# A Mamba block with experts on one core: the front's convolution put on TensorE, stores by parts, and one subtraction moved from POOL to VectorE

## The chip, the core and the metric

The kernel runs on one core of a Trainium2 chip. A core has five engines, each with its own instruction queue: TensorE (PE in the rows; PEld is its weight loads), VectorE (DVE), ScalarE (ACT), GpSimd (POOL) and SyncE (SP), which here only issues DMAs. They wait for one another by semaphores. SBUF is the working memory of 128 partitions; TensorE writes into PSUM, eight banks of 128x512 f32. The metric is the time of one execution in microseconds (us) on the device; lower is better.

## The reference, cut to what matters

The input x is (4, 1024, 128). First a Mamba block, then a layer norm, then four expert layers (4 experts, two chosen per token) and another norm. Only the start of the Mamba block concerns this change:

```python
xn = (x - mu) * rsqrt(var + 1e-05) * ln_w + ln_b
xi, z = split(xn @ W_in, 2)              # 256 channels each
xc = causal depthwise convolution of xi over time, 4 taps   # per channel
u = silu(xc + conv_b)
x_dbl = u @ W_xproj                      # dt_r (8), B (64), C (64)
delta = softplus(dt_r @ W_dt + b_dt)
# then, step by step over time, for every channel d and state n:
#   h = h * exp(delta * A) + (delta * u) * B ;  y = sum_n h * C
y = (y + u * D) * silu(z);  out = x + y @ W_out
```

A depthwise convolution has one weight per channel and tap: xc[t, d] is the sum over j of w[d, j] * xi[t - 3 + j, d].

## The kernel before

The program has three stages: the front (about 210 us), which computes u, silu(z), delta, delta*u, B and C for all tokens and stores them in DRAM; the scan stage, in which VectorE runs 512 scans of 128x1040 elements, with ScalarE and TensorE preparing their inputs; and the expert layers.

**The front** works on items: item k is one batch row's 512 tokens (`TT`), there are 8 (`ITEMS`, `LAST` = 7), and buffers are doubled, `bb = k % 2`. Channels lie on the partitions in two halves of 128 (`HALVES`). Each engine has its own list of work, written out by hand in the order in which it is to run; the loop over k is unrolled. Per item:

- VectorE: moments of x (`input_moments`), normalising it (`input_norm`); `convolve`: for each tap and half one 128x512 instruction, 8 in all (L1298 for tap 0, L1300 for the others), then the last three columns are copied to the front of the buffer `xi` as the next tile's history (L1311), or zeroed (L1313) where the row starts anew; `steps(k-1)`: delta and delta*u (L1319, 1322, 1324); `remainder(k-1)` (L1329, 1331); relu of the softplus argument (L1367), the copy of C (L1373), 1+exp (L1376), its rounding error (L1378), B's high part and its rest (L1385, 1387). The loop's order is: convolve, moments(k+2), steps(k-1), norm(k+2), remainder(k-1), relu, C, softplus, B.
- TensorE: `turn_x` transposes xn (L1015), `inner` multiplies with W_in's first 256 columns (L1024), `gate_of` with the others (L1033); x_dbl = first part of the projection, 72 rows (L1058); `turn_du` transposes delta*u (L1044); `v` is dt_r @ W_dt (L1067); B by token (L1073). Order in the loop: x_dbl(k), turn_du(k-1), v(k), B(k), gate_of(k+1), turn_x(k+2), inner(k+2). Operands are f32; the trace shows two records for each f32 matmul of 512 columns.
- ScalarE: `take_xnT` evacuates the transposed xn with the norm's scale and bias (L842), `take_xi` evacuates inner's result (L850); silu(z) (L877), u = silu(convolution + bias) in two halves (L882), first part of delta (L857), dt_r (L889), first part of delta*u (L862), abs (L897), exp (L901), second part (L867), logarithm (L905). Silu, exp and logarithm need different tables: three table loads an item.
- POOL: the power -0.5 of the norm (L629); `last_part(k-1)` (L674); middle and low part of B (L700, 702); and some clearing of the scan stage's buffers.
- SP: the DMAs, in a written order, too.

**Parts.** delta and delta*u (128x2048 f32 together) are stored as three bf16 numbers that add up to the f32: part 0 is the rounded value (ScalarE), `rest` what is left of it (VectorE), part 1 the rounded rest (ScalarE), part 2 is rest minus part 1 (POOL, L674). Semaphores `a_p0`, `a_p1`, `a_p2` count the items whose part is done. `store_parts(k)` waits for part 2 and then issues 12 DMAs of 256 KB: pairs 0, 1, 2 are part 0, pairs 3 and 4 part 1, pair 5 part 2, each pair for delta (`dl_d`) and delta*u (`du_d`). In item k's turn SP does: load x(k+3), store u and silu(z), store C (`c_d`), store_parts(k-1), store B's six pairs. `a_rows[bb]` counts the landed stores; the first scan of the second block (L1439) and buffer reuse wait for it.

**Waits around the change.** The convolution waits for `a_xi` and, two items later, for `a_u` (its output buffer `conv`); u waits for `a_conv`; take_xi for `a_padded`; x_dbl (L1056) for `a_u`; turn_x(k) for C and dt_r of item k-2, whose PSUM bank it reuses; inner(k) also for `a_brest` of item k-2 (the bank of B); gate_of(k) for `a_rest` of item k-2.

Of the kernel before, what the change touches and what calls it, by code (L numbers as in the profile page):

```python
# [11 lines left out]
P = 128  # L12
# [32 lines left out]
def build(nc, x, vecs, chan, a_log, ident, w_in, w_xproj, w_dt, w_out,  # L45
# [18 lines left out]
    with ctx:  # L64
# [96 lines left out]
        wdt_s = take(DI)  # L161
        assert at_[0] <= GD * SEG
# [7 lines left out]
        dd, rest, slip, lg, sz_s, conv, part, b_part = ([None, None] for _ in range(8))  # L170
# [19 lines left out]
        xnT = [take(TT) for _ in range(2)]  # L190
# [10 lines left out]
        xi = [take(HALVES, KC - 1 + TT) for _ in range(2)]  # L201
# [3 lines left out]
        conv = [take(HALVES, TT) for _ in range(2)]  # L205
# [69 lines left out]
        a_padded = sem("a_padded")  # L275
# [9 lines left out]
        a_xi = sem("a_xi")  # L285
        a_pad = sem("a_pad")
        a_conv = sem("a_conv")
# [23 lines left out]
        a_tap = sem("a_tap")  # L311
# [133 lines left out]
        def _(sp):  # L445
# [17 lines left out]
            load_x(0)  # L463
            load_x(1)
# [47 lines left out]
            for k in range(ITEMS):  # L512
# [26 lines left out]
                if k > 0:  # L539
                    store_parts(k - 1)  # L540
# [4 lines left out]
            store_parts(LAST)  # L545
# [71 lines left out]
        def _(pool):  # L617
            for bb in range(2):
                last = nc.gpsimd.memset(xi[bb][:, :, 0:KC - 1], 0.0)
# [56 lines left out]
            for k in range(ITEMS):  # L676
# [7 lines left out]
                if k == LAST:  # L684
# [4 lines left out]
                    pool.wait_ge(a_conv, ITEMS)  # L689
# [6 lines left out]
                if k > 0:  # L696
                    last_part(k - 1)
# [134 lines left out]
        def _(act):  # L832
# [4 lines left out]
            def take_xnT(k):  # L837
# [7 lines left out]
            def take_xi(k):  # L845
                bb = k % 2
                act.wait_ge(a_xip, k + 1)
                if k > 1:
                    act.wait_ge(a_padded, k - 1)
                nc.scalar.activation(xi[bb][:, :, KC - 1:], PS[:, 4 * bb:4 * bb + 2, :], ACT.Identity).then_inc(a_xi, 1)  # L850
# [857 lines left out]
```

## Time and profile before

| | us |
|---|---|
| three runs, median (lowest to highest) | 2373.51 (2368.64 to 2374.96) |
| the profiled execution | 2374.5 |
| its span, first to last instruction | 2372.7 |
| front, to the first scan | 213 |
| VectorE / TensorE / ScalarE / POOL busy, whole span | 2068.1 / 2152.9 / 1520.5 / 977.3 |

The profile is of one execution. It lists each instruction with its engine, its line, output and inputs, and the idle time before it with the engine that ended it; merged rows carry a count. Idle time of an engine that is not the bound costs nothing; busy shares over the whole span mix three stages with different limits, so the front has to be read by itself.

### The profile page before, as it was taken

How to read it: one execution, taken by the hardware profiler on the slowest of the kernel's cores; microseconds unless marked ns; L12 is line 12 of the kernel's file. 1: busy time of each engine (PE TensorE's matmuls, PEld its weight loads, DVE VectorE, ACT ScalarE, POOL GpSimd, SP SyncE). 2: the span in 40 equal slices, each digit the busy share in tenths (PEclk: the TensorE clock that was granted, in tenths of full speed). 3: DMA queues.
4: the chain of work that ended last, by engine and by line, in shares of the span. 5: the costliest groups of instructions: out<-in, count | busy, mean ns of one | idle time of the engine just before them, and what ended most of it. 6: DMA issues, size and time to landing. Idle time of an engine off the chain costs nothing. (4 is left out here: it accounts for less than half of the span.)

```text
span 2372.7 us, 49889 instructions
## 1 busy us (share of the span) xinstructions
PE 2152.9 (91%) x16864; PEld 1275.1 (54%) x16864; DVE 2068.1 (87%) x2937; ACT 1520.5 (64%) x1795; POOL 977.3 (41%) x475
## 2 busy tenths in 40 slices
PE   6675999999999999999999965999999999989987
PEld 3331333333333333333333324888899989989876
DVE  7987999999999999999999956777877787787776
ACT  5666888888888888888888841343344334434332
POOL 4325344444434434344343424444444544444342
PEclk7665999999999999999999986999999999999998
DMA  4777212212222122221222231000100020000000
GB/s 114 224 225 222 49 40 49 45 40 44 43 45 46 39 44 44 45 46 38 47 45 42 46 104 52 1 0 0 36 1 0 1 72 1 0 1 6 9 4 18
DMA packets 354411, 114.38 MB, mean 48 GB/s; under 512 B 282968, under 2 KB 345056, under 8 KB 354080
## 3 DMA queue, kind: packets, MB, share of 16 engines
q1 hardware_dynamic: 349584, 110.26, 19.0%
q10 hardware_dynamic: 4752, 3.15, 0.4%
q8 instruction: 43, 0.70, 0.1%
q14 instruction: 32, 0.26, 0.0%
HBM read 67.45 MB, written 45.88 MB: 48 GB/s over the span
## 5 line engine op out<-in xcount | busy, mean ns | idle before, releaser
L1442 DVE TENSOR_TENSOR_SCAN arena<-behind 128x1040 f32<-128x1040 f32 x512 | 1156.9, 2309 | 9.8 <-ACT behind L927 6.2
L997 ACT ACTIVATE arena<-PS,arena 128x512 f32<-128x512 f32 x512 | 348.3, 689 | 544.7 <-PE PS L1210 543.8
L917 ACT ACTIVATE behind<-PS 128x1024 f32<-128x1024 f32 x512 | 526.7, 1029 | 133.8 <-DVE arena L1442 101.1
L1126 PE MATMUL PS<-arena 128*32 128x128 f32 x8192 | 566.1, 406 | 1.8 <-DVE arena L1442 1.8
L927 ACT ACTIVATE behind<-PS 128x1024 f32<-128x1024 f32 x512 | 539.2, 1053 | 7.5 <-PE PS L1109 3.8
L1222 PE MATMUL PS<-arena 128*128 128x128 f32 x4096 | 483.8, 278 | 23.2 <-DVE arena L1591 23.0
L1222 PEld LDWEIGHTS PS<-arena 128*128 128x128 f32 x4096 | 480.5, 195 | 34.4 <-DVE arena L1591 22.7
L715 POOL COPY behind<-carry 128x64 f32<-128x64 f32 x128 | 209.7, 1639 | 514.7 <-DVE arena L1442 374.0
L1210 PE MATMUL PS<-parts_xh,parts_w 128*128 128x512 f32 x1536 | 391.1, 409 | 25.8 <-DVE parts_w L1468 15.3
L1126 PEld LDWEIGHTS PS<-arena 128*32 128x32 f32 x8192 | 235.4, 119 | 290.7 <-issue 212.6
L1109 PE MATMUL PS<-arena 96*128 96x512 bf16 x1024 | 314.9, 390 | 53.8 <-ACT behind L927 35.1
L1210 PEld LDWEIGHTS PS<-parts_xh,parts_w 128*128 128x128 f32 x1536 | 292.2, 196 | 86.2 <-DVE parts_w L1468 15.9
L1096 PE MATMUL PS<-arena,Ast 96*128 96x512 bf16 x1024 | 315.1, 390 | 3.9 <-ACT behind L917 3.9
L1503 DVE SCALAR_TENSOR_TENSOR arena<-arena 128x128 f32<-128x128 f32 x164 | 189.3, 1215 | 46.0 <-POOL arena L629 46.0
L1109 PEld LDWEIGHTS PS<-arena 96*128 96x128 bf16 x1024 | 67.5, 98 | 266.6 <-ACT behind L927 249.3
L781 POOL TENSOR_TENSOR arena<-euler,arena 128x16 f32<-128x16 f32 x32 | 92.6, 2894 | 220.3 <-DVE arena L1532 220.3
L1096 PEld LDWEIGHTS PS<-arena,Ast 96*128 96x128 bf16 x1024 | 58.6, 98 | 230.8 <-ACT behind L917 198.9
L1591 DVE SCALAR_TENSOR_TENSOR arena<-PS,arena 128x128 f32 (+1 forms) x512 | 144.0, 344 | 28.9 <-PE PS L1222 19.2
L629 POOL TENSOR_TENSOR arena<-arena,neg_half 128x4 f32<-128x4 f32 x49 | 53.9, 1101 | 241.5 <-DVE arena L1268 241.5
L789 POOL TENSOR_TENSOR arena<-arena 128x2048 f32<-128x2048 f32 x32 | 147.4, 4606 | 12.8 <-POOL arena L629 12.8
L798 POOL TENSOR_TENSOR arena<-arena 128x2048 f32<-128x2048 f32 x32 | 115.6, 3612 | 77.8 <-DVE arena L1562 75.3
L729 POOL COPY arena<-arena 64x64 f32<-64x64 f32 x64 | 129.8, 2028 | 11.8 <-POOL behind L715 9.7
(120 smaller groups left out, 1451.7 us busy)
## 6 DMA issues: line engine op xcount, KB each, us to landing
dl_d<-arena SPq DMA_DIRECT2D x48, 256.0 KB, 3.5
du_d<-arena SPq DMA_DIRECT2D x48, 256.0 KB, 3.6
arena<-dl_d SPq DMA_DIRECT2D x512, 24.0 KB
arena<-b_d SPq DMA_DIRECT2D x64, 192.0 KB
arena<-du_d SPq DMA_DIRECT2D x512, 24.0 KB
b_d<-arena SPq DMA_DIRECT2D x48, 128.0 KB, 2.9
u_d<-behind SPq DMA_DIRECT2D x8, 512.0 KB, 3.7
sz_d<-arena SPq DMA_DIRECT2D x8, 512.0 KB, 4.7
```

The costliest lines, as they stand in the source:

```text
L715: nc.gpsimd.tensor_copy(seg(dB[:, G_])[:, :, 0], carry[:, pair, d:d + GD]).then_inc(slot_ready, 1)
L789: nc.gpsimd.tensor_tensor(scored, X[:, bass.ds(g * GT, GT), :].unsqueeze(2).broadcast_to([P, GT, E, H]), rw_s[:, bass.ds(l, 1)].broadcast_ ...
L917: nc.scalar.activation(seg(dA[:, half])[:, :, 1:], PS[:, 0:2, :].rearrange("p j (i t) -> p (j i) t", t=TC), ACT.Exp).then_inc(exp_done, 1)
L927: nc.scalar.activation(seg(dB[:, G_])[:, :, 1 + 2 * OCT * r:1 + 2 * OCT * (r + 1)], PS[:, 2:4, :].rearrange("p o (t d) -> p d (o t)", d=GD ...
L997: nc.scalar.activation(hT[:, e % 2, c], PS[:, HIDDEN[(GT * e + c) % 3], :], ACT.Gelu, bias=bias1[:, lp, e * GT + c:e * GT + c + 1]).then_i ...
L1096: last = nc.tensor.matmul(PS[:, j, :], Ast[0:ROWS, kk * (DB // GI) + 2 * q + j, :], rhs_d[kk][0:ROWS, 2 * q + j].rearrange("r i t -> r (i ...
L1109: last = nc.tensor.matmul(PS[:, 2 + oct_ % 2, :], Bst[kk][0:ROWS, oct_, :], rhs_u[kk][0:ROWS, oct_, :, G_ * GD:(G_ + 1) * GD], start=True, ...
L1126: last = nc.tensor.matmul(PS[32 * j:32 * j + 32, 4 + kk, 0:DB], cd[:, pair, j, 32 * i:32 * i + 32], seg(hb[kk])[:, :, 1 + 16 * j + i], sta ...
L1210: last = nc.tensor.matmul(PS[:, HIDDEN[(GT * e + c) % 3], :], w1p[:, lp, part_w, e, c * P:(c + 1) * P], xhT[:, gp, part_x], start=(part_w ...
L1222: last = nc.tensor.matmul(PS[:, 2 + e % 2, s * P:(s + 1) * P], hT[:, e % 2, c, s * P:(s + 1) * P], w2_s[:, lp, e * GT + c], start=(c == 0) ...
L1442: nc.vector.tensor_tensor_scan(hb[kk][:, q * QD * SEG:(q + 1) * QD * SEG], dA[:, q % 2], dB[:, G_, lo:lo + QD * SEG], 0.0, ALU.mult, ALU.a ...
L1503: last = nc.vector.scalar_tensor_tensor(dst(s), src(s), mv[:, s, 0:1], rs[:, s:s + 1].broadcast_to([P, H]), ALU.subtract, ALU.mult)
```

## The change

- `convolve`, `take_xi` and their buffers go. The convolution is folded into the projection: `wtap[:, t]` = W_in's first 256 columns times tap t of each output channel, four weight sets made once by VectorE; the taps come in as a new input, repeated on all 128 partitions (128x1024 f32, 512 KB). `inner(k, h)` adds four matmuls on the transposed xn, shifted by one column each, into one PSUM bank. xnT gets three columns of history in front, which ScalarE fills before it takes the next xnT (a copy, or zeros).
- `inner` is split: its first half stands after turn_du(k-1), its second after v(k), for item k+1, one item later than before.
- u is taken by ScalarE straight out of PSUM, ahead of silu(z).
- SP stores each part when it is ready; part 0's six DMAs stand ahead of the store of C.
- `last_part(k-1)` is done by VectorE at the end of its turn, but for the last item, which stays on POOL.

```diff
@@ SP
-            def store_parts(k):
+            def store_part(k, w):
                 it, bb = k // 2, k % 2
-                sp.wait_ge(a_p2, k + 1)
-                for p in range(PAIRS):
-                    src = part[bb][X_PART[p]]
+                sp.wait_ge((a_p0, a_p1, a_p2)[w], k + 1)
+                for p in [p for p in range(PAIRS) if X_PART[p] == w]:
+                    src = part[bb][w]
...
             load_x(0)
+            sp.dma_start(taps_s.rearrange("p t d -> p (t d)"), taps).then_inc(taps_in, 16)
             load_x(1)
...
+                if k > 0:
+                    store_part(k - 1, 0)
                 sp.wait_ge(a_bc, k + 1)
                 sp.dma_start(c_d[it, bb], bc_t[bb][0:N]).then_inc(c_stored[bb], 16)
...
                 if k > 0:
-                    store_parts(k - 1)
+                    store_part(k - 1, 1)
+                    store_part(k - 1, 2)
...
-            store_parts(LAST)
+            for w in range(PARTS):
+                store_part(LAST, w)
@@ POOL
-                if k > 0:
-                    last_part(k - 1)
@@ ACT
                 if k > 1:
                     act.wait_ge(a_zp, k - 1)
-                nc.scalar.activation(xnT[bb], PS[:, 4 * bb, :], ACT.Identity, bias=vecs_s[:, 1:2],
+                    if k // 2 % 2:
+                        nc.scalar.activation(xnT[bb][:, 0:KC - 1], xnT[bb][:, TT:], ACT.Identity).then_inc(a_halo, 1)
+                        act.wait_ge(a_halo, k // 4 * 2 + bb + 1)
+                    else:
+                        nc.scalar.activation(xnT[bb][:, 0:KC - 1], ident_s[:, 0:KC - 1], ACT.Identity, scale=0.0)
+                nc.scalar.activation(xnT[bb][:, KC - 1:], PS[:, 4 * bb, :], ACT.Identity, bias=vecs_s[:, 1:2],
                                      scale=vecs_s[:, 0:1]).then_inc(a_xnT, 1)
...
             for k in range(2):
                 take_xnT(k)
-                take_xi(k)
             for k in range(ITEMS):
                 bb = k % 2
                 if k > 1:
                     act.wait_ge(a_stored[bb], A_STORES * (k // 2))
+                    act.wait_ge(a_du, k - 1)
+                act.wait_ge(a_xip, HALVES * (k + 1))
+                for h in range(HALVES):
+                    last = nc.scalar.activation(u_s[bb][:, h], PS[:, 4 * bb + h, :], ACT.Silu,
+                                                bias=chan_s[:, h, KC:KC + 1])
+                last.then_inc(a_u, 1)
                 act.wait_ge(a_zp, k + 1)
                 nc.scalar.activation(sz_s[bb], PS[:, 4 * bb + 2:4 * bb + 4, :], ACT.Silu).then_inc(a_sz, 1)
-                act.wait_ge(a_conv, k + 1)
-                if k > 1:
-                    act.wait_ge(a_du, k - 1)
-                for h in range(HALVES):
-                    last = nc.scalar.activation(u_s[bb][:, h], conv[bb][:, h], ACT.Silu, bias=chan_s[:, h, KC:KC + 1])
-                last.then_inc(a_u, 1)
-                if 0 < k < LAST:
-                    take_xi(k + 1)
@@ PE
-            def inner(k):
+            def inner(k, h):
                 bb = k % 2
-                pe.wait_ge(a_xnT, k + 1)
-                if k > 1:
+                if h == 0:
+                    pe.wait_ge(a_xnT, k + 1)
+                elif k > 1:
                     pe.wait_ge(a_brest, k - 1)
-                for h in range(HALVES):
-                    last = nc.tensor.matmul(PS[:, 4 * bb + h, :], win_s[:, h * P:(h + 1) * P], xnT[bb],
-                                            start=True, stop=True)
+                for t in range(KC):
+                    last = nc.tensor.matmul(PS[:, 4 * bb + h, :], wtap[:, t, h * P:(h + 1) * P],
+                                            xnT[bb][:, t:t + TT], start=(t == 0), stop=(t == KC - 1))
                 last.then_inc(a_xip, 1)
...
-            for k in range(2):
-                turn_x(k)
-                inner(k)
+            pe.wait_ge(a_pad, 1)
+            pe.wait_ge(a_wtap, KC)
+            turn_x(0)
+            for h in range(HALVES):
+                inner(0, h)
             gate_of(0)
+            turn_x(1)
...
                     turn_du(k - 1)
+                if k < LAST:
+                    inner(k + 1, 0)
...
                 last.then_inc(a_v, 1)
+                if k < LAST:
+                    inner(k + 1, 1)
...
                 if k < ITEMS - 2:
                     turn_x(k + 2)
-                    inner(k + 2)
@@ DVE
+            dve.wait_ge(weights, WEIGHTS)
+            dve.wait_ge(taps_in, 16)
+            for t in range(KC):
+                nc.vector.tensor_tensor(wtap[:, t], win_s[:, 0:DI], taps_s[:, t], ALU.mult).then_inc(a_wtap, 1)
...
-                convolve(k)
...
+                if k > 0:
+                    dve.wait_ge(a_p1, k)
+                    nc.vector.tensor_tensor(part[1 - bb][2], rest[1 - bb], part[1 - bb][1], ALU.subtract
+                                            ).then_inc(a_p2, 1)
             steps(LAST)
```

## Rows read from the trace of the kernel before

**Rows 1.** Busy time of the engines, clock and DMA in one item's stretch
```profile
core 0: us, PE busy (x) PEld busy (x) DVE busy (x) ACT busy (x) POOL busy (x), PEclk, DMA share, GB/s
106.00:130.00 24.00, 16.79 (x44) 8.11 (x44) 21.37 (x35) 15.74 (x17) 7.10 (x5) 0.64 0.78 226
```

**Rows 2.** VectorE in order of time: start, length, line, output<-inputs, count, idle before
```profile
106.72 3.69 DVE L1298 TENSOR_SCALAR arena<-arena,chan_s 128x512 f32<-128x512 f32 x2
110.44 4.60 DVE L1300 SCALAR_TENSOR_TENSOR arena<-arena,chan_s 128x512 f32<-128x512 f32 x6
...
123.25 1.22 DVE L1329 TENSOR_TENSOR arena<-arena 128x1024 f32<-128x1024 f32 x1 [1.82 <-ACT arena L862]
...
130.15 0.42 DVE L1387 TENSOR_TENSOR behind<-PS,arena 128x256 f32<-128x256 f32 x1
130.49 3.53 DVE L1298 TENSOR_SCALAR arena<-arena,chan_s 128x512 f32<-128x512 f32 x1
...
134.59 1.01 DVE L1300 SCALAR_TENSOR_TENSOR arena<-arena,chan_s 128x512 f32<-128x512 f32 x1
```

**Rows 3.** ScalarE in order of time, the same item
```profile
115.08 1.33 ACT L882 ACTIVATE behind<-arena,chan_s 128x512 f32<-128x512 f32 x2 [4.00 <-DVE arena L1300]
...
124.17 1.27 ACT L897 ACTIVATE arena<-PS,chan_s 128x512 f32<-128x512 f32 x2 [0.95 <-PE PS L1067]
125.45 1.28 ACT L901 ACT_TABLE_LOAD   x1
126.74 1.06 ACT L901 ACTIVATE arena<-arena 128x1024 f32<-128x1024 f32 x1
127.70 1.89 ACT L867 ACTIVATE arena<-arena 128x2048 bf16<-128x2048 f32 x1
...
131.87 0.76 ACT L842 ACTIVATE arena<-PS,vecs_s 128x512 f32<-128x512 f32 x1
...
139.20 1.33 ACT L882 ACTIVATE behind<-arena,chan_s 128x512 f32<-128x512 f32 x2 [4.23 <-DVE arena L1300]
```

**Rows 4.** TensorE in order of time, the same item
```profile
116.47 3.69 PE L1058 MATMUL PS<-behind 128*72 128x512 f32 x4 [3.89 <-ACT behind L882]
120.55 1.61 PE L1044 MATMUL PS<-ident_s,arena 128*128 128x128 f32 x8 [0.40 <-DVE arena L1324]
122.09 1.98 PE L1067 MATMUL PS<-behind 8*128 8x512 f32 x4
124.00 2.70 PE L1073 MATMUL PS<-behind 128*128 128x64 f32 x16
126.49 2.94 PE L1033 MATMUL PS<-arena,behind 128*128 128x512 f32 x4
129.27 0.60 PE L1015 MATMUL PS<-ident_s,arena 128*128 128x128 f32 x4
132.69 3.78 PE L1024 MATMUL PS<-arena,behind 128*128 128x512 f32 x4 [2.82 <-ACT arena L842]
```

**Rows 5.** POOL: its third part, and B's middle part
```profile
129.68 4.06 POOL L674 TENSOR_TENSOR arena<-arena 128x2048 bf16<-128x2048 f32 x1 [10.93 <-ACT arena L867]
133.68 0.60 POOL L700 CAST arena<-behind 128x256 bf16<-128x256 f32 x1
```

**Rows 6.** The start of the front: TensorE, then ScalarE
```profile
8.70 1.11 PE L1015 MATMUL PS<-ident_s,arena 128*128 128x128 f32 x4 [8.70 <-DMA lb_s<-in_ln_b]
...
16.24 1.98 PE L1024 MATMUL PS<-arena,behind 128*128 128x512 f32 x4 [0.93 <-ACT arena L842]
...
21.52 1.32 ACT L882 ACTIVATE behind<-arena,chan_s 128x512 f32<-128x512 f32 x2
...
41.08 1.33 ACT L882 ACTIVATE behind<-arena,chan_s 128x512 f32<-128x512 f32 x2 [1.39 <-DVE arena L1300]
```

**Rows 7.** The end of the front: ScalarE's last u, VectorE's second block
```profile
186.72 1.33 ACT L882 ACTIVATE behind<-arena,chan_s 128x512 f32<-128x512 f32 x2 [4.89 <-DVE arena L1300]
...
238.25 22.26 DVE L1442 TENSOR_TENSOR_SCAN arena<-behind 128x1040 f32<-128x1040 f32 x10 [1.09 <-DMA du_d<-arena]
```

More of the change, by code:

```diff
@@ L42, with build @@
 NG = NT // GT
[L45 removed]
+def build(nc, x, vecs, chan, taps, a_log, ident, w_in, w_xproj, w_dt, w_out,
           router_w, router_b, ln_g, ln_b, w1, b1, w2, b2, out):
@@ L161, in build @@
         wdt_s = take(DI)
+        wtap = take(KC, DI)
         assert at_[0] <= GD * SEG
@@ L169, in build @@
         space[0], limit[0] = arena, ARENA
-        dd, rest, slip, lg, sz_s, conv, part, b_part = ([None, None] for _ in range(8))
+        dd, rest, slip, lg, sz_s, part, b_part = ([None, None] for _ in range(7))
         at_[0] = 0
@@ L189, in build @@
         xn = [take(4, H) for _ in range(2)]
-        xnT = [take(TT) for _ in range(2)]
         sz_s[0] = take(HALVES, TT)
@@ L200, in build @@
         at_[0] = LOWER + HB
-        xi = [take(HALVES, KC - 1 + TT) for _ in range(2)]
+        xnT = [take(KC - 1 + TT) for _ in range(2)]
         sz_s[1] = take(HALVES, TT)
@@ L204, in build @@
         at_[0] = LOWER + HB + RD
-        conv = [take(HALVES, TT) for _ in range(2)]
+        taps_s = take(KC, DI)
         slip[0] = take(HALVES, TT)
@@ L618, in _ @@
             for bb in range(2):
-                last = nc.gpsimd.memset(xi[bb][:, :, 0:KC - 1], 0.0)
+                last = nc.gpsimd.memset(xnT[bb][:, 0:KC - 1], 0.0)
             last.then_inc(a_pad, 1)
@@ L1032, in gate_of @@
                 for h in range(HALVES):
-                    last = nc.tensor.matmul(PS[:, 4 * bb + 2 + h, :], win_s[:, (2 + h) * P:(3 + h) * P], xnT[bb],
+                    last = nc.tensor.matmul(PS[:, 4 * bb + 2 + h, :], win_s[:, (2 + h) * P:(3 + h) * P], xnT[bb][:, KC - 1:],
                                             start=True, stop=True)
@@ L1287, in input_norm @@
                 scaled(lambda s: xt[bb][:, s], mv_a[:, bb], rs_a[:, bb], lambda s: xn[bb][:, s], 4).then_inc(a_xn, 1)
-            def convolve(k):
-                bb = k % 2
-                dve.wait_ge(a_xi, k + 1)
-                if k > 1:
-                    dve.wait_ge(a_u, k - 1)
-                for t in range(KC):
-                    for h in range(HALVES):
-                        tap = chan_s[:, h, t:t + 1]
-                        if t == 0:
-                            last = nc.vector.tensor_scalar(conv[bb][:, h], xi[bb][:, h, t:t + TT], tap, None, ALU.mult)
-                        else:
-                            last = nc.vector.scalar_tensor_tensor(conv[bb][:, h], xi[bb][:, h, t:t + TT], tap,
-                                                                  conv[bb][:, h], ALU.mult, ALU.add)
-                    if t < KC - 1:
-                        last.then_inc(a_tap, 1)
-                        dve.wait_ge(a_tap, k * (KC - 1) + t + 1)
-                    else:
-                        last.then_inc(a_conv, 1)
-                dve.wait_ge(a_conv, k + 1)
-                pad = xi[bb][:, :, 0:KC - 1]
-                if k // 2 % 2 == 0:
-                    nc.vector.tensor_copy(pad, xi[bb][:, :, TT:]).then_inc(a_padded, 1)
-                elif k < ITEMS - 2:
-                    nc.vector.memset(pad, 0.0).then_inc(a_padded, 1)
             def steps(k):
@@ L1685 @@
                                 halves(L0_attn_b_dt), halves(L0_attn_D)], 2),
+        "taps": np.concatenate([f(L0_attn_conv_w).reshape(DI, KC).T.reshape(1, KC * DI)] * P, 0),
         "a_log": f(L0_attn_A_log),
```

18 lines of the change are left out of this document (4 added, 14 removed).

## The prediction

> **What bounds the kernel now.** I read the page's slices first (the front is the first tenth of the span), then the busy time of each engine in one item's stretch, then that item on VectorE, ScalarE and TensorE in order of time. An item is one 512-token tile; there are eight, k = 0 to 7, and the middle ones take 24.1 us each, the spacing of the two u activations in [rows 3] (115.08 and 139.20). In that stretch VectorE is busy 21.4 us of 24, ScalarE 15.7, TensorE 16.8, at a mean granted clock of 0.64, which is mostly the lower of its levels (1.2 of 2.4 GHz) [rows 1]. VectorE is the bound: its only long idle stretch is 1.8 us [rows 2], and ScalarE's u waits 4.0 to 4.2 us for the last tap of the convolution [rows 3]. The convolution costs it 3.7 + 4.6 us in an item [rows 2]. Its first two instructions, single-input operations on 128x512, are stretched: one of them alone took 3.53 us and ended at 134.02, beside POOL's third part, which ran from 129.68 to 133.74 [rows 2, 5]. TensorE waits 2.8 us for xnT and about 4 us for u [rows 4]. After the eighth item the front runs out into the scans; there only the second block's first scan waits for the stores, by 1.09 us [rows 7]. From then on VectorE scans without a gap (10 in 22.3 us [rows 7]) that the front could fill, so whatever brings that scan forward moves the end by as much.
>
> **The change part by part.** *VectorE loses* the convolution and the pad copy, 3.7 + 4.6 + 0.1 = 8.4 us an item, the copy of six columns taken at 0.1, *and gains* the third part: one subtraction of 128x2048, f32 and bf16 in, bf16 out. The nearest row is the same kind of subtraction on 128x1024, 1.22 us [rows 2], so 2.3 us (twice 1.22 less one start-up; above, 2.44). Busy time goes from 21.4 to about 15.3 us: VectorE stops being the bound, if nothing stretches the new instruction.
>
> *POOL* loses 4.06 us an item [rows 5], and with it what held VectorE's single-input operations. It keeps the middle and low part of B. These now start when the third part does, on the other engine. A three-operand instruction of VectorE beside such a POOL operation took 1.01 us where six of its kind took 4.60 together [rows 2]; so I add 0.3 us, 2.6 in all. In the schedule below VectorE has about 1 us of slack there: behind the third part are queued the moments of item k+2 and steps(k), and ScalarE's next wait for delta is also a wait for x_dbl. Cost: nothing up to about 3 us of length, then one for one. The Trainium skill, page SBUF — State Buffer, section Who interferes with whom, says more: the ports that VectorE and GpSimd share are an exclusive lock, and a VectorE instruction with two SBUF inputs contends with a GpSimd instruction that reads SBUF. By that rule the third part could wait out a whole POOL operation rather than 0.3 us, which is the third rival; the 3.53 us in [rows 2] agrees with a lock, and the 1.01 us speaks for a short wait only.
>
> *TensorE gains* three more matmuls for each half, each two records: inner goes from 4 records to 16. Four records took 3.78 us at the low level and 1.98 us at the high one, each with the drain of the last [rows 4, 6]; so one half of an item, 8 records, takes 7.2 or 3.7 us. The idle time of 2.8 us in front of inner and the 4 us before x_dbl are to be judged by the new chain, and that is two legs.
>
> Leg A, from the start of x_dbl(k) to the end of v(k), on TensorE: x_dbl 3.7 (it stands behind an idle stretch, as now, and ran at the low level), turn_du 1.6, the first half of inner(k+1), v 2.0 [rows 4]. In the trace v already runs at the high level, after 5.3 us of x_dbl and turn_du; so I take the half of inner at 3.7. Sum 11.0, less three overlaps of about 0.2 between listed ends and next starts = 10.4. Where the clock is still high at x_dbl this would be 1.7 less. I take 10.0.
>
> Leg B, from there to the next x_dbl, on ScalarE: abs 1.27, table 1.28 (the load is as long each of the three times), exp 0.96 to the next start, second part 1.92, table 1.28, logarithm 0.96 (an instruction like exp's), the new copy of three columns, xnT 0.77, table 1.28, u 1.33 [rows 3]. The copy of three columns has no row; it is bounded by nothing and by the 0.76 us of xnT's 512 columns [rows 3], and a line through that row and exp's (1024 columns, 1.06) leaves 0.46 for no columns at all, of which 0.1 overlaps with the next instruction; as xnT is the dearer form (it reads a scale and a bias), I take 0.25. Sum 11.3. Beside it TensorE does the second half of inner 3.7, B 2.7, the gate 2.9, turn_x 0.6 [rows 4] = 9.9, which fits, though barely: xnT(k+2) waits for that turn_x, and u(k+1) stands behind xnT on ScalarE. So xi's evacuation (1.0 us) goes, and the wait for the convolution goes, but what was hidden beneath it, three table loads included, now lies on the path. The spacing is 10.0 + 11.3 = 21.3 us; I take 21.4. VectorE (15.3) and DMA (0.78 of 24 = 18.7 us of traffic, unchanged in bytes [rows 1]) are below it.
>
> *The start* is later. u(0) begins at 21.52 [rows 6]. New: the taps, 512 KB, are queued ahead of the second x and of the weights, at 225 GB/s [rows 1] up to 2.3 us; TensorE's first work at 8.70 [rows 6] would slip by 0 to 2.3, I take 1.0. The four products for wtap then cost VectorE 4 x 0.42 (the 128x256 row of [rows 2]) = 1.7. From 11.4: turn_x 1.1, xnT 0.8, sixteen records of which four to eight low = 9.2 to 10.9, I take 10; gate 2.0; turn_x(1) 1.0; xnT(1) 0.8, because ScalarE now takes xnT(0) and xnT(1) before anything else; table 1.3. That is 28.4, less overlaps of 0.7 = 27.7: 6.2 us later. The first spacing was 19.6 (21.52 to 41.08 [rows 6]), as item 0 has no predecessor's parts; I take 20.0.
>
> *SP.* A part's stores are released one by one: six after the first part, four after the second, two after the third. The first six are moved ahead of c_d; what is queued behind their wait is c_d and everything after it. c_d is waited for two items later, so this costs nothing. At the end only two stores are left after POOL's last third part, instead of twelve; the 1.09 us wait of block 1 [rows 7] goes. What is late next there are the eight scans of block 0, which do not change.
>
> *Sum.* u(0) to u(7) now: 186.72 - 21.52 = 165.2 us [rows 6, 7]. After: 20.0 + 6 x 21.4 = 148.4. So -16.8, start +6.2, end -1.1: -11.7 us. The profiled execution took 2374.5 (span 2372.7), so 2362.8; the median of the three runs is 1.0 below the profiled one, so 2362.0 when rounded. Scans and expert layers are untouched.
>
> **The rivals.** *Slower: the low clock reaches the convolution.* If leg A's half of inner runs at the low level (7.2 in place of 3.7), leg A is 13.9, the spacing 25.2 to 25.4, and the total 20 + 6 x 25.3 - 165.2 + 6.2 - 1.1 = +11.7: 2386. The place is the first half of inner, behind the idle stretch before x_dbl; the point from which it decides is a spacing of 23.4 us (leg A of 12.1), where the whole change is nothing. For it: after its idle stretch of 2.8 us the inner at 132.69 ran wholly low [rows 4], and an idle stretch of 3.5 us before x_dbl stays (xnT, table, u). Against it: the work after it is denser than before, with 8 records in one piece twice an item, and v was at the high level. 0.13.
>
> *Faster: the clock stays high.* x_dbl 2.0, turn_du 1.0, leg A 8.2, spacing 19.5 to 20; total 20 + 6 x 19.8 - 165.2 + 6.2 - 1.1 = -21.3: 2353. For it: TensorE is now busy some 18 of 20 us; against it: the idle stretch. 0.12.
>
> *The third part is stretched.* If it waits for both of POOL's operations on B, each about as long as the 0.60 us one [rows 5], it is 2.3 + 1.2 = 3.5, 0.5 beyond the slack, in about seven items -4 of the gain; a stretch to the 4.06 us that POOL needed would give back 1 more an item. 2366 to 2371. 0.12.
>
> *Nothing is gained.* The chain closes another way, for instance because SP's stores or the loads in items 4 and 7 set the spacing at about 23.4: 2374. 0.10.
>
> **How the numbers follow.** The forecast of -7 to -16 us has 0.53 and is the likeliest, 2362. A measurement of this kernel tells about 0.3%, 7.1 us, from no change. Faster by more: 0.53 + 0.12 and a part of the third rival, 0.70. Within: the rest of the third and the fourth, 0.17. Slower: 0.13. The range has to leave out no more than 2 in 10: from 2350 (the high-clock case and 3 us of spread, the runs lying 6.3 apart) to 2376 (no gain, and spread), which leaves out the slow rival and little else.
>
> **What would show it.** Right: no convolution on VectorE, its busy share of an item near 15 us; u starts 21 to 22 us apart; a third part of 2.3 to 2.6 us; u(0) at 27 to 28; ScalarE from abs to u without a wait but for turn_x's; block 1's first scan at about 226 and waiting for no store. Wrong: inner's first half above 5 us in most items; a third part above 3; ScalarE waiting for delta longer than for x_dbl; TensorE waiting for wtap beyond 13; or a spacing that follows from SP.

## The result, and the profile after

The changed kernel takes 2363.67 us, the median of 7 runs (2362.76 to 2364.74); the kernel before took 2371.76, the median of 7 runs beside them (2368.64 to 2374.96). The ratio is 0.9965, 95% interval 0.9956 to 0.9975: faster by 8.1 us, where 11.7 were forecast. The profiled execution took 2364.13 us, its span is 2362.3 (before 2372.7).

The page of the changed kernel: the engines' busy time, then VectorE's busy share and the granted clock in 40 slices.

```profile
PE 2162.7 (92%) x16960; PEld 1276.8 (54%) x16960; DVE 2026.2 (86%) x2878; ACT 1513.0 (64%) x1793; POOL 960.9 (41%) x468
...
DVE  4768999999999999999999956777877787787776
...
PEclk9895999999999999999999986999999999999999
```

VectorE lost 41.9 us of work (it had 2068.1), all in the front, the first four digits. The clock there is 9, 8, 9, 5; the kernel before had 7, 6, 6, 5.

The same stretch as [rows 1], and one item from u(4) to u(5) (columns as there):

```profile
106.00:130.00 24.00, 20.27 (x76) 10.95 (x75) 17.63 (x30) 17.48 (x19) 4.97 (x3) 0.93 0.85 237
113.01:134.29 21.28, 17.42 (x56) 8.64 (x56) 15.28 (x28) 14.74 (x16) 4.94 (x3) 0.92 0.94 262
```

An item takes 21.3 us, and VectorE is busy for 15.3 of them, where it was 21.4 of 24. No engine is busy all the time: two of them take turns. ScalarE over the same item, in order of time, answers to [rows 3]:

```profile
103.13 1.26 ACT L893 ACTIVATE arena<-PS,chan_s 128x512 f32<-128x512 f32 x2 [4.68 <-PE PS L1069]
104.41 1.28 ACT L897 ACT_TABLE_LOAD   x1
...
106.67 1.90 ACT L866 ACTIVATE arena<-arena 128x2048 bf16<-128x2048 f32 x1
...
110.85 0.18 ACT L847 ACTIVATE arena<-ident_s 128x3 f32<-128x3 f32 x1
110.94 0.76 ACT L848 ACTIVATE arena<-PS,vecs_s 128x512 f32<-128x512 f32 x1
111.72 1.28 ACT L877 ACT_TABLE_LOAD   x1
113.01 1.26 ACT L877 ACTIVATE behind<-PS,chan_s 128x512 f32<-128x512 f32 x2
```

From abs (103.13) to the end of u (114.27) it waits for nothing: that is leg B of the prediction, 11.1 us. The copy of the three history columns costs 0.1 us on the path. Its one long wait, 4.68 us, is for v. TensorE answers to [rows 4]:

```profile
101.05 1.98 PE L1069 MATMUL PS<-behind 8*128 8x512 f32 x4
102.96 3.70 PE L1021 MATMUL PS<-arena,behind 128*128 128x512 f32 x8
106.50 1.89 PE L1077 MATMUL PS<-behind 128*128 128x64 f32 x16
108.23 1.94 PE L1030 MATMUL PS<-arena,behind 128*128 128x512 f32 x4
110.00 0.60 PE L1011 MATMUL PS<-ident_s,arena 128*128 128x128 f32 x4
114.33 3.13 PE L1058 MATMUL PS<-behind 128*72 128x512 f32 x4 [3.73 <-ACT behind L877]
117.25 1.57 PE L1041 MATMUL PS<-ident_s,arena 128*128 128x128 f32 x8
```

It idles 3.73 us for u, then runs x_dbl mostly at the low level (3.13 us), turn_du, inner's first half and v, which ended at 124.17: leg A, 9.8 us. Inner's second half, B and the gate are at the high level, under ScalarE's leg.

The start, TensorE; it answers to [rows 6]:

```profile
12.95 1.09 PE L1011 MATMUL PS<-ident_s,arena 128*128 128x128 f32 x4 [12.95 <-DVE behind L1319]
14.91 9.33 PE L1021 MATMUL PS<-arena,behind 128*128 128x512 f32 x16 [0.87 <-ACT arena L848]
24.08 1.88 PE L1030 MATMUL PS<-arena,behind 128*128 128x512 f32 x4
25.79 0.60 PE L1011 MATMUL PS<-ident_s,arena 128*128 128x128 f32 x4
```

And the end of the front, VectorE's scans; it answers to [rows 7]:

```profile
203.41 2.33 DVE L1425 TENSOR_TENSOR_SCAN arena<-behind 128x1040 f32<-128x1040 f32 x1 [3.83 <-ACT behind L923]
...
211.81 24.39 DVE L1425 TENSOR_TENSOR_SCAN arena<-behind 128x1040 f32<-128x1040 f32 x10 [1.59 <-ACT behind L913]
236.82 44.42 DVE L1425 TENSOR_TENSOR_SCAN arena<-behind 128x1040 f32<-128x1040 f32 x20 [0.62 <-ACT behind L923]
```

The first scan came at 203.41 instead of 213.23. Block 1's first scan (block: eight scans) is the seventh of the ten, at 227.26, and waits for no store; four scans later, at 236.82, there is a new wait of 0.62 us for ScalarE.

The marks that the next section compares, in us from the start of each profiled execution. Gate operation is the first of VectorE's two 128x128 products with a PSUM input behind the 32nd scan, at 291.45 in the kernel before.

| kernel | median of runs | u(0) | u(7) | first scan | block 1 | gate operation |
|---|---|---|---|---|---|---|
| before | 2371.76 | 21.52 | 186.72 | 213.23 | 238.25 | 291.45 |
| after | 2363.67 | 28.52 | 177.07 | 203.41 | 227.26 | 281.16 |
| after, part on POOL | 2367.04 | 28.78 | 176.25 | 204.56 | 228.41 | 282.31 |
| after, stores at once | 2368.70 | 27.80 | 176.75 | 206.97 | 232.80 | 286.00 |
| convolution alone | 2371.62 | 28.31 | 177.24 | 208.77 | 235.16 | 288.36 |
| before, part on VectorE | 2371.67 | 21.20 | 181.68 | 207.95 | 232.03 | 285.88 |
| before, stores by parts | 2372.67 | 23.15 | 186.97 | 213.48 | 237.56 | 291.52 |
| before, both of these | 2370.91 | 21.43 | 185.71 | 211.01 | 235.10 | 288.74 |

One execution is not the median: the profiled one of before is 2.7 us above it, that of the before with the part on VectorE 2.5 below. The items of the kernels with the convolution on VectorE vary with the clock, and their runs lie 4 to 6.5 us apart. What counts as worth something below goes by the medians; the marks show where it happens.

### The profile page after: what moved, and what is told of

Its sections match the earlier page's. It is cut to its first block and busy times, and to the rows that moved or that the text cites. A ratio compares the mean times of both kernels' runs of the same rounds, so it can differ in the third digit from the quotient of the medians.

```text
span 2362.3 us, 49990 instructions
## 1 busy us (share of the span) xinstructions
PE 2162.7 (92%) x16960; PEld 1276.8 (54%) x16960; DVE 2026.2 (86%) x2878; ACT 1513.0 (64%) x1793; POOL 960.9 (41%) x468
## 5 line engine op out<-in xcount | busy, mean ns | idle before, releaser
L1574 DVE SCALAR_TENSOR_TENSOR arena<-PS,arena 128x128 f32 (+1 forms) x512 | 144.1, 344 | 26.5 <-PE PS L1225 16.6
```

## The experiments

### Undo one small part of the change each

The third part back on POOL:

```diff
@@ POOL
                     nc.gpsimd.memset(words(rhs_u[1]), 0.0).then_inc(clear_u[1], 1)
+                if k > 0:
+                    last_part(k - 1)
@@ VectorE
-                if k > 0:
-                    dve.wait_ge(a_p1, k)
-                    nc.vector.tensor_tensor(part[1 - bb][2], rest[1 - bb], part[1 - bb][1], ALU.subtract
-                                            ).then_inc(a_p2, 1)
```

> The changed kernel, but with the third part of items 0 to 6 made by POOL again, as before. Theory A (the gain comes from the convolution's leaving VectorE; what sets an item now is the loop of TensorE and ScalarE, and VectorE has a slack of over 1 us): POOL's 4.1 us ends at about the time at which VectorE's steps could start anyway, so the time stays at 2364, at most 2366; u starts stay 21 to 22 us apart. Theory B (the gain comes from freeing VectorE of POOL's hold on the ports): VectorE's three subtractions behind it, each with two SBUF inputs, are held, each item gets 2 us or more longer, and half or more of the 8 us of gain goes: 2368 to 2372.

Measured: 2367.04 us (2366.06 to 2368.15, 11 runs), ratio to before 0.9982 [0.9973, 0.9991]: 3.4 us of the gain is gone. Neither theory's time came (2364 to 2366, 2368 to 2372). The items are as long as after (u(0) to u(7) 147.5 us, after 148.6), so Theory A is right about them. The loss arises behind them: POOL makes item 6's third part, 4.0 us, after it has cleared the scan buffers (195.28), so B's parts and the copies ahead of the first scan are late, and the first scan comes 1.15 us later; the gate operation as well. Another 1.6 us is lost in the scans, which do the same work as in the changed kernel: once in every 32 scans VectorE stands still before the same scan, 0.36 us the first time and 0.09 to 0.11 each time after that.

```profile
292.07 2.32 DVE L1423 TENSOR_TENSOR_SCAN arena<-behind 128x1040 f32<-128x1040 f32 x1 [0.36 <-issue]
```

"issue" means that the engine waited for nothing that the profile shows. By the last scan the distance to after has grown from 1.15 to 2.73 us; at the end of the execution it is 2.2. The stretches are in the traces of exactly two kernels, this one and the convolution alone below, and not in that of the kernel before, which has its third part on POOL, too. Their cause is not shown; they are no part of what the third part's place was meant to change.

The twelve stores together, behind the third part, at their old place:

```diff
@@ SP
-                if k > 0:
-                    store_part(k - 1, 0)
                 sp.wait_ge(a_bc, k + 1)
...
-                    store_part(k - 1, 1)
-                    store_part(k - 1, 2)
+                    sp.wait_ge(a_p2, k)
+                    for w in range(PARTS):
+                        store_part(k - 1, w)
...
+            sp.wait_ge(a_p2, ITEMS)
             for w in range(PARTS):
                 store_part(LAST, w)
```

> The changed kernel, but with all twelve stores of an item issued together when its third part is done, at the old place behind the store of C. Theory A: only the end feels it. Block 1's first scan waits for the last stores again, but the changed kernel gave back about 0.7 us of what it won there, so 0 to 1.5 us slower: 2364 to 2365.5. Rival: SP's queue is close to an item's spacing of 21 us (15 to 16 us of issues) and bunched stores push u's and B's stores late, so the reuse waits of ScalarE on landed stores grow: 2367 or more, with ScalarE waiting for DMAs inside the items.

Measured: 2368.70 us (2367.47 to 2369.87, 11 runs), ratio 0.9986 [0.9977, 0.9995]: 5.0 us of the gain is gone, again with items as long as after (149.0 us), and with the first scan 3.6 us and block 1's 5.5 us later. The rival's time came, but not its place: only the end feels it, as Theory A had it, and by far more than its 1.5 us.

### One part of the change alone, and the two small ones together

On the kernel before, the third part on VectorE (the lines above), then the stores by parts, then both; and the convolution alone, which is the changed kernel with both undone.

> The kernel before, with one edit: the third part of items 0 to 6 is made by VectorE at the end of its turn. VectorE stays the bound. Its convolution's first pair falls from 3.7 to 4.1 us to about 1.1 (nothing of POOL beside it), the third part adds 2.3. Theory A: the item gets 0.3 to 0.6 us shorter, in seven items 2 to 4 us: 2368 to 2370 where before is 2372. Theory B (this move is the main part of the gain): 2364 to 2366. A third outcome, if the new instruction is held by POOL's work on B: no gain or 2 us slower.

> The kernel before, with one edit: the stores released by parts, part 0 ahead of the store of C. Theory A: VectorE bounds the items, so nothing changes in them; the last stores land earlier and the 1.09 us wait of block 1 goes: 2370.5 to 2371.5 where before is 2372, not to be told from it. Rival: the stores' order is worth more, since SP reached its last stores late: 2368 or less.

> The convolution on TensorE alone: the third part on POOL again and all twelve stores of an item at once. If the two others add up with it (3.4 and 5.0 us lost one at a time), the whole gain of 8 us is gone: 2371 to 2373, and the convolution's move alone is worth nothing at the end, although its items are 21 to 22 us apart instead of 24. If both losses are the same one (the last items' stores and the clearing of the scan stage's buffers queued behind one another), 2368 to 2370.

> The kernel before with the third part on VectorE and stores by parts, the convolution still on VectorE: the one combination of the three edits that is missing. Theory: the two small edits shorten the run-out after the last u, and this is worth something only behind items that TensorE and ScalarE set; while VectorE sets the items, the 2.3 us of the third part lie on its path and take back what the run-out gains. Then the time is the before's, 2370 to 2373, with u starts about 23 us apart as in the run with the third part alone. Rival: the two edits need only each other (the two bottlenecks of the run-out, POOL's third part and SP's twelve stores, lie one behind the other, so that removing one alone shows nothing): then 2364 to 2367 without the convolution moved at all, and the move of the convolution is worth nothing by itself in any combination.

Measured, with the two above, all eight combinations:

| | neither | part on VectorE | stores by parts | both |
|---|---|---|---|---|
| convolution on VectorE | 2371.8 | 2371.7 | 2372.7 | 2370.9 |
| convolution on TensorE | 2371.6 | 2368.7 | 2367.0 | 2363.7 |
| the move is worth | -0.1 | -3.0 | -5.6 | -7.2 |

The ratios of the upper row and of the convolution alone are 1.0001, 1.0001, 0.9996 and 0.9997, each within 0.001 of 1 at 95%. So the convolution's move, which is the whole mechanism of the prediction, is worth nothing by itself, though its items are 21.3 us long like those of after. The two small edits are worth nothing by themselves or together while the convolution is on VectorE. Only all three give the 8 us. The intervals of single entries are 2 us either way, so that the share of each small edit (3.4 and 5.0) is less sure than this pattern. Two entries, 2371.6 and 2367.0, hold the 1.6 us of stretches in the scans. Without them the convolution's move alone would be worth about 1.7 us, and the third part's move 1.8 in place of 3.4: an estimate, from one trace of each. For the third part alone 2368 to 2370 was expected. Its trace does have items shorter by 0.5 us, but it lies 2.5 us below the median, which shows no gain. The other three forecasts hold within the noise.

The traces say where most of the convolution's 9.5 us is lost: u(7) comes that much earlier, the first scan only 4.5 and block 1 only 3.1; the stretches in the scans then take the 1.6. VectorE's scans with the convolution alone:

```profile
208.77 2.33 DVE L1423 TENSOR_TENSOR_SCAN arena<-behind 128x1040 f32<-128x1040 f32 x1 [12.29 <-POOL behind L718]
...
235.16 53.28 DVE L1423 TENSOR_TENSOR_SCAN arena<-behind 128x1040 f32<-128x1040 f32 x24 [2.46 <-DMA du_d<-arena]
```

The first waits for POOL, the second for stores of delta*u. POOL, the same kernel:

```profile
173.63 4.07 POOL L678 TENSOR_TENSOR arena<-arena 128x2048 bf16<-128x2048 f32 x1 [15.77 <-ACT arena L868]
...
196.50 3.51 POOL L694 MEMSET arena<- 128x4096 f32 x1 [12.43 <-DMA sz_d<-arena]
199.95 3.51 POOL L698 MEMSET arena<- 128x4096 f32 x1
203.42 3.81 POOL L678 TENSOR_TENSOR arena<-arena 128x2048 bf16<-128x2048 f32 x1
```

POOL has to clear the buffer in which silu(z) of item 7 lies, and that waits until this is stored. SP issues that store in this order (the start and length of each issue):

```profile
177.72 0.38 SPq L457 DMA_DIRECT2D dl_d<-arena  x1
...
185.78 0.80 SPq L459 DMA_DIRECT2D du_d<-arena  x1
186.62 4.18 SPq L545 DMA_DIRECT2D b_d<-arena  x6
190.91 0.52 SPq L519 DMA_DIRECT2D u_d<-behind  x1
191.47 0.52 SPq L519 DMA_DIRECT2D sz_d<-arena  x1
```

The third part of item 5 ends at 177.70. Behind it SP has twelve stores (8.9 us: the first four issues take 0.38 to 0.57, each of the others about 0.80), B's six (4.2) and u: silu(z) is issued at 191.47, and POOL's clearing begins at 196.50, 18.8 us behind the first of the twelve. In the kernel before these were 181.28 and 200.10, and with the twelve stores at once 176.27 and 195.08, 18.8 again. This chain of SP had the same length in all three and hangs on the third part of item 5, not on u(7). The convolution's move brought that third part forward by 3.6 us and not by 9.5. In the kernel before it began 9.5 us ahead of u(7) (177.20 and 186.72), with the convolution between the two; now it begins 3.6 us ahead (173.63 and 177.24). The 5.9 us between are won for u(7) alone. In the changed kernel only the last two stores stand behind the third part:

```profile
174.96 0.54 SPq L459 DMA_DIRECT2D du_d<-arena  x1
176.59 0.37 SPq L457 DMA_DIRECT2D dl_d<-arena  x1
177.01 0.49 SPq L459 DMA_DIRECT2D du_d<-arena  x1
178.42 3.38 SPq L546 DMA_DIRECT2D b_d<-arena  x6
181.90 0.49 SPq L519 DMA_DIRECT2D u_d<-behind  x1
182.43 0.49 SPq L519 DMA_DIRECT2D sz_d<-arena  x1
```

Silu(z) is issued at 182.43, 9.0 us earlier, and POOL's clearing begins at 187.06. What sets the first scan now is ScalarE's chain behind u(7). While the convolution is on VectorE, that chain (26.3 to 26.5 us from u(7) to the first scan in three of these kernels, 25.3 in the fourth) ends last anyway, so an earlier store changes nothing there: with stores by parts on the kernel before, POOL's clearing began 6.9 us earlier (193.24), and the first scan was at 213.48 as against 213.23.

### Which leg sets the item: ScalarE's second part ahead of abs

```diff
@@ ScalarE
                 if k > 0:
                     first_part_du(k - 1)
+                    second_part(k - 1)
...
-                if k > 0:
-                    second_part(k - 1)
                 act.wait_ge(a_onep, k + 1)
```

> The changed kernel with ScalarE's second part (1.9 us) moved out of the stretch behind v: it stands ahead of abs, in the 4.4 us in which ScalarE waits for v. Theory A (two chains of almost one length close the loop: ScalarE from abs to xnT, and TensorE's second inner half, B, gate and turn_x, after which xnT, a table and u still follow): TensorE's is then the longer one at once, so only 0.3 to 0.6 us an item are won: 2360 to 2362. Rival (ScalarE alone is the bound, as the prediction's leg B had it): 1.9 us an item, 12 us in all: 2351 to 2353.

Measured: 2363.74 us (2362.65 to 2365.77, 6 runs), ratio 0.9968 [0.9956, 0.9979]: no difference from after, and above both ranges. It takes 1.9 us out of leg B and puts them where ScalarE waited for v. But xnT now waits, where before it did not:

```profile
101.22 1.26 ACT L894 ACTIVATE arena<-PS,chan_s 128x512 f32<-128x512 f32 x2
...
108.73 0.21 ACT L847 ACTIVATE arena<-ident_s 128x3 f32<-128x3 f32 x1 [1.51 <-PE PS L1010]
```

Line 1010 is turn_x. The prediction said of TensorE's 9.9 us under leg B that they fit barely. They are 7.6 (103.03 to 110.60 in the changed kernel, at the high level of the clock), and turn_x ends only 0.25 us before ScalarE asks for it. So they end last as soon as ScalarE is 1.9 us shorter, and the first six spacings are only 0.1 us shorter each. Theory A had the mechanism right and priced it too high.

The last item has no turn_x and no xnT. There 3.0 us are won, and u(7) comes 4.1 us earlier than after (172.98), but the first scan only 0.2 (203.19). Behind u(7) turn_du waits 2.36 us for delta*u. Then abs, whose input v had ended at 183.26, stands behind the second part, which has itself waited for VectorE:

```profile
183.14 1.91 ACT L866 ACTIVATE arena<-arena 128x2048 bf16<-128x2048 f32 x1 [2.42 <-DVE arena L1307]
184.96 1.25 ACT L894 ACTIVATE arena<-PS,chan_s 128x512 f32<-128x512 f32 x2
```

In the changed kernel this abs began at 185.03. From u(7) to the first scan it takes 30.2 us here, and 26.3 after. The two kernels below that have the second part ahead of abs take 30.2 as well, the two without it 26.3 and 26.4: this move costs 3.8 us at the end.

### Take xnT off leg B

xnT(k+1) is taken after silu(z)(k), where ScalarE waits anyway, and only xnT(0) ahead of the loop:

```diff
@@ ScalarE
-            for k in range(2):
-                take_xnT(k)
+            take_xnT(0)
             for k in range(ITEMS):
...
                 nc.scalar.activation(sz_s[bb], PS[:, 4 * bb + 2:4 * bb + 4, :], ACT.Silu).then_inc(a_sz, 1)
+                if k < LAST:
+                    take_xnT(k + 1)
...
-                if k < ITEMS - 2:
-                    take_xnT(k + 2)
```

> The changed kernel with xnT(k+1) taken behind u(k) and silu(z)(k) instead of xnT(k+2) ahead of u(k+1), also at the start. Theory A: u no longer stands behind turn_x and xnT. About 1 us an item goes from ScalarE's leg (20.2 in place of 21.2), and at the start u(0) no longer waits for gate, turn_x(1) and xnT(1), 4 us earlier: 2364 less 11 = 2352 to 2355. Rival (TensorE's work and its low clock fill the loop, whatever the order): only the start is won, 2359 to 2361.

Measured: 2352.80 us (2347.69 to 2355.76, 6 runs), ratio 0.9921 [0.9909, 0.9933]: 10.9 us below after. Theory A holds. In its profiled execution (2348.97, 3.8 below the median), u(0) comes at 24.19 (after 28.52), u(7) at 161.87 (after 177.07), an item is 20.4 us long in the middle, and the clock was at the high level throughout the items:

```profile
24.00:162.00 138.00, 112.02 (x389) 55.02 (x387) 96.10 (x151) 99.05 (x109) 32.93 (x20) 1.00 0.83 241
```

Four of the six executions took 2352.01 to 2355.76 us, with a mean granted clock of 0.960 to 0.963 over the whole span; this one and one other had 0.967 and 0.968. So the execution at the median probably did not look like this trace, in which the clock stayed high up to 162 us.

Both moves together:

> Both moves of ScalarE's order. Theory A: leg B of ScalarE is 8.4 us, TensorE has 8.1 of work in it and no idle stretch of 3.7 us is left; an item takes 18.5 to 20.5 us, where DMA's 18.7 us and VectorE's 16 to 18 us come next: 2348 to 2354. Rival: the next bound (DMA, or VectorE's chain from delta to the parts) is hit at once, and it is no better than the second move alone, within 2 us.

Measured: 2350.67 us (2349.81 to 2355.71, 4 runs), ratio 0.9911 [0.9897, 0.9926]: 2.1 us less, which the intervals don't separate from the run before. TensorE in it:

```profile
64.32 1.30 PE L1039 MATMUL PS<-ident_s,arena 128*128 128x128 f32 x8 [3.35 <-DVE arena L1299]
65.42 5.09 PE L1019 MATMUL PS<-arena,behind 128*128 128x512 f32 x8
```

turn_du waits 3.35 us for delta*u, and the half of inner behind it takes 5.09 us in place of 3.6; it takes 5.66 and 4.25 in the next two items and 3.60 in the others. This trace is 5.0 us above the kernel's median. The next bound of its items is VectorE's order: third part, moments, and only then the steps that make delta*u.

### VectorE's steps first

On the kernel with xnT moved, and on the one with both moves:

```diff
@@ VectorE
-                if k < ITEMS - 2:
-                    input_moments(k + 2)
                 if k > 0:
                     steps(k - 1)
                 if k < ITEMS - 2:
-                    input_norm(k + 2)
+                    input_moments(k + 2)
                 if k > 0:
                     remainder(k - 1)
+                if k < ITEMS - 2:
+                    input_norm(k + 2)
```

> The run e8_xnT_after_u (2352.8 us), and VectorE makes delta and delta*u (steps) ahead of the moments of item k+2, and the remainder ahead of that item's norm. In e8's trace turn_du waits 1.54 us for delta*u (106.35 us, released by VectorE), because VectorE goes from the third part (to 101.0) to 1.5 us of moments before the steps, though the logarithm had ended at 100.2. Theory (TensorE's leg from x_dbl to v, with VectorE's steps now in it, sets the item together with ScalarE's leg): 1.46 us less an item over 7 items, about -9 with what the run-out keeps: 2343 to 2346, u starts 19.0 us apart. Rival (a wait of the same length turns up at once elsewhere, as when both moves were made together, for instance v before relu, or B's stores): 2350 to 2354, u starts still above 20.

> The run e9_both_moves (2350.7 us), with the same order of VectorE as in e11. In e9's trace turn_du waits 3.35 us for delta*u at 64.32 and the half of inner behind it takes 5.09 us in place of 3.6 (granted clock 0.95 over the items), so there the gap costs twice: the wait and the lower clock. Theory: steps 1.46 us earlier and, with a shorter idle stretch of TensorE, the half of inner back at 3.6 to 3.7: 2.9 us an item where it was low, 1.5 elsewhere, together -9 to -14: 2337 to 2342, granted clock 0.98 or more in the items, and below e11. Rival (ScalarE's second part, ahead of abs, now holds abs back when VectorE has the remainder late): 2345 to 2351, not below e11.

Measured: 2348.47 us (2346.71 to 2348.98, 4 runs), ratio 0.9897 [0.988, 0.9913], and 2350.62 us (2350.29 to 2351.65, 4 runs), ratio 0.9906 [0.9889, 0.9922]. The first is 4.3 us below the run without this order, where 9 were expected, and between the ranges of theory and rival; the intervals of the two ratios touch. It is the fastest kernel of this study, 1.0% below before. The second gains nothing. In the first, the order did what it should: turn_du no longer waits. TensorE with xnT moved, and below it the same place with the steps first:

```profile
102.87 1.94 PE L1057 MATMUL PS<-behind 128*72 128x512 f32 x4 [2.96 <-ACT behind L876]
106.35 1.06 PE L1040 MATMUL PS<-ident_s,arena 128*128 128x128 f32 x8 [1.54 <-DVE arena L1300]
```

```profile
99.93 3.63 PE L1057 MATMUL PS<-behind 128*72 128x512 f32 x4 [2.96 <-ACT behind L876]
103.36 1.08 PE L1040 MATMUL PS<-ident_s,arena 128*128 128x128 f32 x8
```

The idle stretch before x_dbl is 2.96 us in both. With the wait of 1.54 us behind it, x_dbl ran at the high level (1.94 us, granted clock 1.00); without that wait it ran at the low level (3.63 us, granted clock 0.51): 1.69 us more, which takes back the 1.54. It is so in items 3 to 6: 1.94 us in the one, 3.47 to 3.63 in the other; in item 7 both are low (3.4). The middle items are 20.4 us long either way (98.61 to 119.00 here). The gain comes from the first ones, whose x_dbl is still at the high level: u(2) at 58.81 against 60.69 and u(3) at 78.27 against 81.12, the 19 us items of the expectation. So its mechanism held for two items, and then the clock took it back. Of the lead, 0.8 us is there at u(0) already, and at the first scan it is 2.3 (186.06 against 188.31). The traces therefore explain 2.3 us; the rest of the 4.3 lies in the longer executions of the kernel without this order, of which there is no trace. Why the clock stays up across 2.96 us of idling in one order and not in the other was not settled.

With both moves and the steps first, turn_du's wait fell from 3.35 to 2.36 us and the half of inner stayed between the levels in three items (4.88, 4.35 and 4.71). The rival had the second part hold abs back. In the items it does not: the second part waits 2.42 us for VectorE's remainder in each, but v ends later still in three of them (abs waits for it 0.75 to 1.29 us) and at the same time in two others. Behind u(7) it does, as above: u(7) comes at 159.97, as in the kernel without the second part's move (159.78), but the first scan at 190.14 and not at 186.06. These 4.1 us are the whole difference between the two traces (2.2 between the medians): what the second part's move costs is lost behind the items, not in them.

## Why the prediction was right, and where it was not

**The time.** 2362.0 was forecast (the sum gives 2361.8), 2363.67 came, inside the range of 2350 to 2376, and faster by over 0.3% was the likeliest of the three. Of the 3.6 us by which the gain is smaller, 2.2 lie in the reference: the forecast took before's profiled execution as 1.0 above the median, over 7 runs it is 2.7 above, and after's own is 0.5 above. The other 1.3 are terms of the sum. That it held is in part luck: by the runs, the term from which it takes the gain, the items, arrives at the end only through two edits that it priced at nothing and at 1.1 us.

**Items.** u(0) to u(7): forecast 148.4, measured 177.07 - 28.52 = 148.55. Leg A 10.0, measured 9.8: x_dbl 3.13 and not 3.7, the half of inner 3.6 for 3.7. Leg B 11.3, measured 11.1; the copy of three columns 0.1 on the path for 0.25. The runs that change a leg bear the two-leg view out as well: taking xnT off leg B shortened the items, and taking the second part off it did almost nothing to them, because TensorE's part beneath it was then the longer.

**Start.** +6.2 forecast, +7.0 measured. The step that failed is the four products for wtap: 1.41 us as taken (1.7), but they stand behind VectorE's norm of both first items, so turn_x began at 12.95 and not at 11.4; a part of it came back as a shorter inner (9.33 for 10).

**End.** -1.1 forecast; the span gained 0.75 us more than u(7) did (10.4 against 9.65). The store wait of block 1 (1.09 us) went, but a wait of 0.62 us for ScalarE appeared four scans later, for which the prediction has no term.

**What was wrong though the sum held.** The sentence that whatever brings the scans forward moves the end by as much is right for this change (10.3 us at the gate operation, 10.4 at the end); the step from there to u(7) is not. The sum priced stores by parts at "costs nothing" and 1.1 us at the end, and the third part on VectorE only as a cost. Measured, with the convolution moved, they are worth 5.0 and 3.4 us (of the latter, 1.6 are the stretches in the scans, whose cause is open), and without them the 9.5 us of u(7) come to nothing. The mark was the wrong one: two chains lead to the first scan, ScalarE's from u(7) and SP's from the third part of item 5 over the store of silu(z) to POOL's clearing. Both can be read from the trace of before; the prediction read only the first.

**The rivals.** The low clock did not reach the convolution: the first half of inner took 3.60 us in five of the seven items and 3.94 and 3.97 in two, never near 5. The clock did not stay high at x_dbl either (3.13 to 3.69 in the first seven items), though it did in the trace with xnT moved. The stretched third part did not come:

```profile
109.46 2.28 DVE L1370 TENSOR_TENSOR arena<-arena 128x2048 bf16<-128x2048 f32 x1
```

```profile
109.61 2.39 POOL L701 CAST arena<-behind 128x256 bf16<-128x256 f32 x1 [16.69 <-DVE behind L1366]
```

VectorE's instruction came first and was not held; POOL's cast, 0.60 us in [rows 5], was held until it had ended (111.74 and 112.00). The Trainium skill, page SBUF — State Buffer, section Who interferes with whom, calls the shared ports an exclusive lock and says that the order of issue decides who is blocked. The trace agrees: the later one paid, and it had slack. "Nothing is gained" named SP's stores as a cause, and with the convolution alone nothing was gained; but the stores did it behind the loop, while the spacing stayed at 21.3 us and did not go to the rival's 23.4. The two small edits kept it from the whole change. Two prices of rivals are off by a little in their own terms: the slow one is 2386 only from the profiled execution (2385 from the median), and a third part of 4.06 in place of 3.5 us would cost 0.6 more an item, not 1.

**The signs.** VectorE busy 15.3 an item (near 15), u 21.4 apart on the mean from u(1) on, 20.8 to 22.3 singly (21 to 22), third part 2.28 (2.3 to 2.6) and no wait in leg B came as said; u(0) at 28.5 (27 to 28) and block 1's first scan at 227.3 (226) are a little late.

## What to carry to other kernels

Before a gain in a loop is carried to the end, list each chain that leads from the loop to the work behind it, and take as mark the instruction on which each hangs: a queue of stores behind a late part can hold everything that a shorter item gains, and an instruction moved into a loop's idle stretch can stand on the path where the loop ends. Edits that each measure as nothing can be worth the whole gain together, so an edit is judged on the kernel in which its neighbours are already made. When a wait is taken from TensorE, read the granted clock behind the idle stretch again, since it can give the wait back. Compare the times of the profiled executions with their medians before their traces are compared: here one trace was 3.8 us below its kernel's median and another 5.0 above, more than the effects under study.

## What the runs showed of the hardware

- Store issues of 256 KB take SP 0.37 to 0.57 us for the first four and 0.80 from then on when twelve follow one another; split over an item, most take 0.37 to 0.57. The same bytes cost SP less time when the stores are spaced.
- POOL's cast, issued 0.15 us behind a two-input VectorE instruction of 2.28 us, waited for its end: 2.39 us for a cast of 0.60 (or 0.40 alone). POOL's power operation on 128x4 took 1.92 us beside VectorE's steps and 1.01 where VectorE ran no two-input instruction.
- x_dbl, four matmul records behind the same idle stretch of 2.96 us, took 1.94 us in one order of the work (granted clock 1.00) and 3.63 in another (0.51).
- VectorE stood still 0.09 to 0.36 us once in every 32 scans, waiting for nothing that the profile shows, in two of the thirteen kernels; together 1.6 us.
